# When each expert's hidden rows are split in two: ScalarE rounds and VectorE subtracts in the expert's own step instead of one step later

## What is computed

```python
x = x + 0.5 * ffn(layernorm(x))
x = x + attn(layernorm(x))
x = x + 0.5 * ffn(layernorm(x))

def ffn(x):                      # D = 256, E = 8 experts, H = 128, top 2
    scores = sigmoid(x @ gate_W) * route_scale
    gate_full = ...              # the two best scores, normalised; else 0
    h = gelu(einsum('bsd,edh->bseh', x, W1) + b1)
    y = einsum('bseh,ehd->bsed', h, W2) + b2
    return einsum('bse,bsed->bsd', gate_full, y) \
        + gelu(x @ Ws1 + bs1) @ Ws2 + bs2
```

## Time and profile before

| | |
|---|---|
| median of 3 runs | 2441.58 us (2441.37 to 2449.67) |
| profiled execution, its own time | 2440.7 us |
| its span (first to last instruction) | 2438.9 us |
| around the span | 1.8 us |
| granted TensorE clock | 0.998 of full speed |
| first mixture | about 20 to 278 us of the span |
| second mixture | about 2190 to 2436 us of the span |

### The profile page before, as it was taken

The page is one execution under the profiler, slowest core; times in us unless marked ns, Lnnn a source line. Parts: engine busy times, 40 slices in busy tenths (PEclk is TensorE's granted clock), DMA queues, the critical chain, the costliest instruction groups (busy, mean ns, idle before and its releaser), DMA issues.

```text
span 2438.9 us, 46253 instructions
## 1 busy us (share of the span) xinstructions
PE 2382.4 (98%) x14472; PEld 2066.2 (85%) x14472; DVE 1865.4 (76%) x3615; ACT 1693.0 (69%) x2932; POOL 1512.4 (62%) x1536
## 2 busy tenths in 40 slices
PE   8999899999999999999999999999999999999999
PEld 7888778888888888888888888888888879988888
DVE  7887677878878788887878878787887875466675
ACT  4555577878878787877878778787887865443443
POOL 1333378777777777767787777777777754542220
PEclk9999999999999999999999999999999999999999
DMA  4744531222212132221213312122221345431332
GB/s 179 267 160 162 198 113 44 87 80 84 95 44 86 53 97 71 72 95 44 86 61 95 97 41 95 44 86 80 84 95 43 108 156 169 139 116 64 126 130 82
DMA packets 131969, 245.66 MB, mean 101 GB/s; under 512 B 7290, under 2 KB 90132, under 8 KB 120052
## 3 DMA queue, kind: packets, MB, share of 16 engines
q1 hardware_dynamic: 131828, 244.15, 30.8%
HBM read 140.12 MB, written 53.67 MB: 79 GB/s over the span
## 4 chain that ended last, share of the span: by engine, by line
PE 81%; DVE 8%; issue 5%; POOL 2%; ACT 2%; DMA 1%; SPq 0%; DVEq 0%; ACTq 0%; POOLq 0%
PE a_ov L1693 19%; PE a_sc L1657 18%; PE a_tr L1669 18%; PE a_pj L1612 7%; PE a_pj L1621 4%; PE g_acc L963 3%; PE g_hid L921 3%; PE f_acc L963 2%; PE f_hid L921 2%; PE m_proj L2096 1%; POOL m_zin L1948 1%; PE m_hid L2162 1%; DVE f_hp L735 1%; DVE f_gated L730 1%; DVE a_pT L1580 1%
## 5 line engine op out<-in xcount | busy, mean ns | idle before, releaser
L1569 DVE TENSOR_REDUCE a_nmax<-a_sc 128x1 f32<-128x1024 f32 x512 | 626.8, 1224 | 261.6 <-PE a_sc L1657 253.4
L1496 POOL TENSOR_SCALAR a_pr<-a_pr,a_rden 128x1024 f32<-128x1024 f32 x512 | 575.8, 1126 | 260.8 <-DVE a_rden L1574 191.4
L1412 ACT ACTIVATE a_pT<-a_tr 128x512 fp32r<-128x512 f32 x1024 | 560.1, 596 | 208.9 <-PE a_tr L1669 205.0
L1580 DVE TENSOR_TENSOR a_pT<-a_tr,a_pT 128x512 fp32r<-128x512 f32 x1024 | 650.0, 677 | 17.2 <-ACT a_pT L1412 17.2
L1693 PE MATMUL a_ov<-a_pT,a_v_s 128*128 128x512 f32 x2048 | 598.6, 414 | 3.1 <-DVE a_half L1560 2.0
L1418 ACT ACTIVATE a_pr<-a_sc,a_nmax 128x1024 f32<-128x1024 f32 x512 | 573.7, 1120 | 32.8 <-DVE a_nmax L1569 29.3
L1657 PE MATMUL a_sc<-a_k_s,a_q_s 128*128 128x512 f32 x2048 | 554.5, 392 | 3.3 <-DMA a_k_s<-a_k_s 3.3
L1669 PEld LDWEIGHTS a_tr<-f_ident,a_pr 128*128 128x128 f32 x4096 | 474.4, 140 | 92.3 <-DVE a_pT L1580 19.1
L1669 PE MATMUL a_tr<-f_ident,a_pr 128*128 128x128 f32 x4096 | 538.6, 274 | 9.3 <-DVE a_pT L1580 9.1
L1657 PEld LDWEIGHTS a_sc<-a_k_s,a_q_s 128*128 128x128 f32 x2048 | 380.2, 188 | 83.5 <-DMA a_k_s<-a_k_s 3.5
L1693 PEld LDWEIGHTS a_ov<-a_pT,a_v_s 128*128 128x128 f32 x2048 | 346.3, 189 | 53.9 <-issue 4.9
(11 more groups left out here) (252 smaller groups left out, 3220.8 us busy)
## 6 DMA issues: line engine op xcount, KB each, us to landing
a_z_s<-zT SPq DMA_DIRECT2D x32, 1024.0 KB, 7.7
a_k_s<-a_k_s SPq DMA_DIRECT2D x62, 512.0 KB, 5.7
a_wqk_s<-w_split SPq DMA_DIRECT2D x64, 256.0 KB, 3.1
a_v_s<-a_v_b SPq DMA_DIRECT2D x16, 1024.0 KB, 4.5
att<-a_ao SPq DMA_DIRECT2D x32, 512.0 KB, 2.9
m_in<-att SPq DMA_DIRECT2D x16, 1024.0 KB, 6.1
f_gB<-f_gate_rows SPq DMA_DIRECT2D x12, 1024.0 KB, 5.0
g_gB<-g_gate_rows SPq DMA_DIRECT2D x12, 1024.0 KB, 4.7
```

The source lines that it names most:

```text
L1412: act.activation(pT[:, (u // 4) % 2, 0, 4 * part:4 * part + 4, (u % 4) * P:(u % 4 + 1) * P], tr[:, part].rearrange("p (t q) -> p t q", t=4 ...
L1496: pool.tensor_scalar(pr[:, k % NP], pr[:, k % NP], rden[:, k % NP:k % NP + 1], 1.0, ALU.mult, ALU.mult).then_inc(s["normed"], 1)
L1569: dve.tensor_reduce(nmax[:, k % NP:k % NP + 1], sc[:, k % 2], AX.X, ALU.max, negate=True).then_inc(s["negmax"], 1)
L1580: dve.tensor_tensor(to[:, 1], tr[:, part].rearrange("p (t q) -> p t q", t=4), to[:, 0].bitcast(F32), ALU.subtract).then_inc(s["tr_lo"], 1)
```

## The change

ACT's step e becomes: GELU of e, then `hi` of **e** itself, then the other work. The call after the last block goes.

DVE's step e becomes: `gating` of e; `lo` of **e** at once in block 0 and in steps 0, 3 and 8 of the other blocks; then the step's other work; and in the remaining steps (1, 2, 4, 5, 6, 7) `lo` of **e** behind it. Nothing is added or removed; PE's, POOL's and SP's lists stay as they are.

```diff
@@ on_scalar, body
                 act.activation(act_out[:, e % 3], hid[:, (par + e) % 2], ACT.Gelu,
                                bias=b1[:, weights_of(e):weights_of(e) + 1]).then_inc(s["gelu"], 1)
-                if e > 0:
-                    hi(i, e - 1, first)
-                elif not first:
-                    hi(i - 1, E, False)
+                hi(i, e, first)
...
         over_blocks(act, body)
-        hi(NB - 1, E, False)
@@ on_vector, body
                 if e == 1 and not first:
 
                     result(i - 1)
-                if e > 0 and not (tail and first and e == 1):
-                    lo(i, e - 1)
-                elif e == 0 and not first:
-                    lo(i - 1, NE - 1)
+                at_once = first or e in (0, 3, NE - 1)
+                if at_once and not (tail and first and e == 0):
+                    lo(i, e)
...
                 if tail and last and e in SUMS_AT:
                     bias_sum(SUMS_AT[e])
+                if not at_once:
+                    lo(i, e)
         over_blocks(dve, body)
-        lo(NB - 1, E)
```

## The result

The changed kernel is slower: 2466.1 us (median of 4 executions, 2456.01 to 2470.53) against 2444.22 for the kernel before on the same chip (4 executions, 2441.37 to 2449.67). The ratio is 1.0085 with a 95% interval of 1.0064 to 1.0107 (it is estimated from all executions and so is not exactly the quotient of the medians). The forecast was 2458, the range up to 2470. The profiled execution is the shortest of the four, 2456.01 us with a span of 2454.2; that is 15.3 us above that of before, where the sum had +17.1.

A forecast was written before the change was run, and what follows sets the result against it. The prediction took PE, busy for 98% of the span, as the bound; 12 + 4.0 + 2.6 - 2.0 + 1.4 - 0.9 = +17.1 us on 2440.7 gave 2457.8, stated as 2458 us, range 2444 to 2470.

The forecast's parts named there:

- the sum: Whole kernel: 12 + 4.0 + 2.6 - 2.0 + 1.4 - 0.9 = +17.1 us.
- The middle blocks, +12: First mixture, blocks 1 to 6: late `zn_norm` makes PE's transposes of `f_zn` 2.0 us late per block, +12 us.
- the walk: First mixture's middle block followed from the GELU of 3: `z_norm` 2.9 us late, PE's `f_zn` 2.0 us late.
- the lower bound: Middle block: +1.4 us, if DVE's 0.55 us idle before the gating of 4 takes up part of the delay.
- The hand-over prices: Between ACT and DVE: gating to its `hi` 0.79 us, `hi` to its `lo` 0.66 us.
- The wait of the second product of 3 gone: First mixture's middle block: PE's wait for `lo` at this product, 0.82 us before, disappears.
- the rival that the waits simply go: PE's waits for `lo` vanish and nothing replaces them: about 2427 us, or 2413 for all; chance 0.08.
- Block 0, +4.0: First mixture's block 0: every `lo` at once delays DVE, 3.7 us at `gates_up`; +4.0 us, bounds +1.4 and +5.
- Block 7, +2.6: First mixture's block 7: `lo` of 6 and 7 behind `bias_sum`, second product of 8 2.6 us later; bounds 0 and +3.5.
- The second mixture, -1.5 in all: Second mixture, without norms: middle blocks -2.0 us, block 0 +1.4, block 7 -0.9; bounds together -4 and +1.
- 2440.7 + 17.1 [...] or 2458.7 against the median: Whole kernel: adds +17.1 us to the profiled execution, giving 2457.8, or 2458.7 against the median of 2441.58.
- The last rival: Late `hi` delays GELUs or DVE cannot catch up: another 1.3 us in six blocks plus upper edge bounds, 2468 to 2475; chance 0.10.

The follow-up runs named there:

- norms_ahead: Changed kernel with `z_norm` and `zn_norm` ahead of the step's own `hi` on ACT; 2444.77 us, ratio to before 1.0005.
- late_zn: Kernel before, with only `zn_norm` moved from the end of step 7 into step 8; 2453.19 us, ratio to before 1.0048.
- changed_again: Changed kernel run once more, unedited; 2467.85 us, ratio to before 1.0107.
- warm: Changed kernel plus 36 identity transposes on PE ahead of `gates_up` in block 0 of each mixture; 2458.96 us, ratio to before 1.0084.
- best6: Changed kernel, norms before `hi`, old order in both blocks 0 and first mixture's block 7, `lo` of 6 at once; 2443.64 us, ratio to before 1.0005.

## Why the prediction was right, and where it was off

**The middle blocks, +12: right in size and cause.** The new wait at L884 was forecast at 1.5 to 2 us and is 1.64 in block 3, 1.7 at most; the six blocks lost 1.5 to 2.3 us each. norms_ahead removes the loss by moving two norms, late_zn makes it out of nothing but the late norm. Two steps of the walk were each 0.5 us too large: `z_norm` came 2.4 us late, not 2.9, and `zn_norm` 2.8, not 3.3, because DVE's idle time before the gating of 4 shrank from 0.55 us to 0.20 and took up some of the delay. That was named as the lower bound. So in block 3 the transposes come 1.5 us later behind the GELU of 3 (PE's first one after 19.14 us against 17.63), and the block is 1.5 us longer, not 2.0. That the sum comes to 11.7 all the same is owed to blocks 1, 2 and 6, with 2.1 to 2.3 us each; why these lose more was not taken apart, so that the total meets the forecast this closely is in part luck.

**The hand-over prices carried over.** From gating to its `hi` 0.79 us was read once in the earlier trace rows; now it is 0.73 (140.12 to 140.85), and `hi` to `lo` 0.66 (140.85 to 141.51), as forecast.

**"The wait of the second product of 3 gone": right,** but those of 5 (0.44 us) and 6 (0.96, 0.76 before) are there now (with that of 4, 0.68, they make 2.1 us a block in place of 2.4), so the waits for `lo` in the first mixture are still 16.7 us. This is why the rival that the waits simply go failed. The rule of the Trainium skill that stood beside it (Perfetto Trace Analysis, Optimization Strategy: find the semaphore that the full engine waits for and make that dependency start sooner) named the right semaphore; in the first mixture it did not say that 11.6 us of another wait would come in exchange. In the second mixture, which has no norms, it held outside block 0: -2.0 and -1.0.

**Block 0, +4.0: 4.3.** The steps at DVE hold. `gates_up` starts 4.14 us late instead of 1.83:

```profile
56.13 0.99 PE L904 MATMUL f_aux<-f_ident,f_gpad 128*128 128x128 f32 x4 [4.14 <-DVE f_gpad L709]
56.78 2.91 PE L917 MATMUL f_hid<-f_xT,f_w1p 128*128 128x512 f32 x6
```

Counted from the start of the block it comes 3.46 us later (3.7 forecast). What I had not priced stands in the second row: the first product behind the wait takes 2.91 us, not the 1.6 of its neighbours, at a granted clock of 0.66 from 55 to 60 us. So the next second product is 4.3 us late, where PE was to have got 0.8 back, and the further loss forecast at the logits did not come; the two errors cancel.

**Block 7, +2.6: 3.0.** Its weight loads wait 2.46 us at the second product of 4 and 2.05 at that of 7, as in the earlier trace rows. In between they stand 1.86 us ahead of the transposes; the row names no releaser, but the matmul behind it waits 1.68 us for ACT's `f_zn`:

```profile
280.01 1.49 PEld L959 LDWEIGHTS f_acc<-f_w2p,f_hp 128*128 128x128 f32 x12 [2.46 <-DVE f_hp L731]
...
290.67 0.85 PEld L884 LDWEIGHTS f_aux<-f_ident,f_zn 128*128 128x128 f32 x8 [1.86 <-issue]
...
293.57 1.50 PEld L959 LDWEIGHTS f_acc<-f_w2p,f_hp 128*128 128x128 f32 x12 [2.05 <-DVE f_hp L731]
```

Counted from the block's start the second product of 8 comes 3.0 us later (295.62 - 265.76 against 277.30 - 250.46); the forecast had 2.6. The clock has no part in this 3.0: the matmuls behind the first wait ran at 0.66 (280 to 285 us), but changed_again, at 1.00 there, reaches the transposes and the second product of 7 after the same 24.94 and 27.81 us.

**The second mixture, -1.5 in all: -0.6.** The middle (-2.0) and the end (-1.0) are as forecast. Block 0 was mis-sized, +2.4 and not +1.4, by slow matmuls behind a long wait again:

```profile
2240.31 0.66 PE L904 MATMUL g_aux<-f_ident,g_gpad 128*128 128x128 f32 x4 [3.84 <-DVE g_gpad L709]
2240.72 2.81 PE L917 MATMUL g_hid<-g_xT,g_w1p 128*128 128x512 f32 x6
2243.32 2.02 PE L959 MATMUL g_acc<-g_w2p,g_hp 128*128 128x256 f32 x12
```

warm, which fills this wait, brings block 0 down by 0.9 us: this time is the clock's. Without it the block would be at +1.5, so the walk itself was right.

**The median, 8 us above the forecast.** Of these, 2.6 us are in the base: with a fourth execution the median before is 2444.22 us and no longer 2441.58. The other 5.5 are the difference of the medians, 21.9 us where the forecast had 16.4. Here the step that failed is "2440.7 + 17.1 [...] or 2458.7 against the median": it took for granted that the clock of the changed kernel's executions would be that of before. The kernel before has a mean clock of 0.991 to 0.998 over the span in 55 executions; the 8 of the changed kernel have 0.989 to 0.996. A straight line through each kernel's executions falls by about 1.9 us per 0.001 of this clock for both. At 0.996 it gives 2440.6 for before and 2456.9 for the changed kernel, +16.3 us against the sum's +17.1; only one of the changed kernel's eight executions lies at 0.996, so this is an estimate. The remaining 5.6 us of the medians' difference go together with the lower clock of the changed kernel's executions. Some of it lies behind its own long waits. The larger part stands at the start of the attention where two profiles of this kernel can be compared (changed_again, 8.9 of 12.3 us), and why the clock stays low there for so long is open.

**A bound that does not add up.** The last rival went to 2475. Its own terms, 6 x 1.3 us and the upper bounds of block 0, block 7 and the second mixture, give 2457.8 + 7.8 + 1.0 + 0.9 + 2.5 = 2470. Nothing else in the forecast hangs on it.

## What to carry to other kernels

An edit that lets one operand come sooner must be walked through everything that shares the in-order queue with it: here `hi` was moved so that it needed the newest DVE result, and two norms that were left behind it became the bound (+11.7 us in six blocks). Put first in a queue what is ready and wanted soon, and check it in every block: in block 7 the same norm waits for GpSimd, and with the norm in front a ready `hi` stands behind it. Where an order is repeated in two places with different neighbours, forecast them apart: the same edit lost 19 us in one mixture and won 3 in the middle and end of the other. And before you put a loss down to a wait, compare PE's busy time for the same matmuls: in best6 6.3 of 8.0 us were clock and not waiting.

## What the runs showed of the hardware

- Behind a wait of about 4 us PE's matmuls ran slow: first products of 2.91 and 2.81 us instead of 1.63, at a granted clock of 0.66 (55 to 60 us) and 0.83 (2240 to 2250 us); with the wait filled by other matmuls, 1.63. A long wait is not the only place where the clock falls: in best6 it was 0.74 from 160 to 165 us with PE busy for all 5 us, and the only wait for `lo` in the 15 us before was 0.92 us.
- The 3.3 us wait for a DMA at the start of the attention is followed by a low clock in the kernel before (0.66, 290 to 295 us), in the changed one (0.77, 310 to 315 us) and in changed_again, where it stays at 0.50 from 315 to 335 us.
- The same program is granted a different clock from execution to execution: at the start of the attention a window of 10 us at 0.50 (1.2 GHz) in one and at 0.89 to 1.00 in another. The time goes with it, by about 1.9 us per 0.001 of the span's mean clock, and differs by up to 14.5 us between two executions of the changed kernel. A difference of 0.5% between medians of a few executions is not safe without the clocks beside it.
